# A Fourier tokenizer: last channel stored in four rings, table rows numbered by ring, chunks in a new order

## The reference, cut to what matters

```python
f = fftshift(fft2(images))                  # 64 images, 3 channels, 224 x 224
power = abs(f cropped to 192 x 192 about the centre)
idx = argsort(distance from the centre)     # 36864 points, stable
ps = power[:, :, idx].reshape(64, 3, 16, 2304)        # 16 bins by radius
tokens = einsum('bnf,ef->bne', ps of all channels per bin, W) + b
tokens = [cls, tokens] + sinusoidal positions         # 17 tokens of 192
h = layernorm(h + attention(h)); h = layernorm(h + ffn with 8 experts, top 2)
```

## Time and profile before

| | us |
|---|---|
| median of three runs | 814.05 |
| the profiled execution | 816.31 |
| its span, first to last instruction | 814.4 |
| what lies around the span | 1.9 |
| PE / DVE / POOL / ACT busy | 699.3 / 533.5 / 428.7 / 440.0 |
| transform ends (last root) | 277.2 |
| first gather, last gather issued | 287.0, 504.1 |

### The profile page before, as it was taken

One profiled execution on the slowest core, in us unless ns is written; L12 is line 12 of the kernel. 1 busy time (PEld: TensorE's weight loads), 2 busy tenths in 40 slices (PEclk: granted clock), 3 DMA queues, 4 the chain that ended last, 5 costly groups with the idle time before them and its releaser, 6 DMA issues. The chain is left out here.

```text
span 814.4 us, 22164 instructions
## 1 busy us (share of the span) xinstructions
PE 699.3 (86%) x8537; PEld 595.3 (73%) x8537; DVE 533.5 (66%) x1058; ACT 440.0 (54%) x864; POOL 428.7 (53%) x375
## 2 busy tenths in 40 slices
PE   4999999999999225788888888998899889999980
PEld 4788888888888124688787888677467677999970
DVE  3899999999999312465555555697668773555544
ACT  1788888888888512354444454232453221766640
POOL 4666677767676243777777776000200202567751
PEclk9999999999999657889999999999899965999995
DMA  9874569865996296565554554200000684233424
GB/s 244 202 194 143 149 180 259 231 186 139 266 268 269 49 228 181 152 169 155 152 145 141 147 150 136 81 2 1 1 2 2 254 252 149 37 58 58 58 29 126
DMA packets 78519, 114.90 MB, mean 141 GB/s; under 512 B 8791, under 2 KB 58108, under 8 KB 78076
## 3 DMA queue, kind: packets, MB, share of 16 engines
q1 hardware_dynamic: 61246, 76.80, 33.5%
q0 software_dynamic: 14336, 35.40, 16.8%
q10 hardware_dynamic: 2880, 1.90, 0.7%
HBM read 91.83 MB, written 22.25 MB: 140 GB/s over the span
## 5 line engine op out<-in xcount | busy, mean ns | idle before, releaser
L598 PE MATMUL psum<-power,tT 128*128 128x192 f32 x864 | 162.4, 345 | 65.4 <-DVE tT L725 65.1
L598 PEld LDWEIGHTS psum<-power,tT 128*128 128x128 f32 x864 | 148.1, 200 | 76.3 <-DVE tT L725 41.4
L539 POOL DMA_INDIRECT rows<-power_table,rank_row x144 | 146.4, 1017 | 65.9 <-issue 54.0
L725 DVE SCALAR_TENSOR_TENSOR tT<-rows,swaps,scaled 128x384 f32<-128x384 f32 x144 | 82.8, 616 | 120.7 <-ACT scaled L653 120.1
L331 PE MATMUL ps<-dft,fold 112*64 112x97 f32 (+1 forms) x3072 | 147.2, 249 | 11.6 <-POOL fold L295 11.6
L653 ACT ACTIVATE scaled<-rows,swaps 128x384 f32<-128x384 f32 x144 | 80.3, 606 | 138.8 <-DMA rows<-power_table,rank_row 135.5
L331 PEld LDWEIGHTS ps<-dft,fold 112*64 112x64 f32 (+1 forms) x3072 | 141.9, 131 | 16.6 <-issue 11.9
L302 POOL TENSOR_TENSOR ss<-uv 97x388 f32<-97x388 f32 x96 | 82.3, 880 | 76.7 <-ACT uv L373 76.7
L405 DVE TENSOR_TENSOR folded<-ps,far 112x388 f32<-112x388 f32 x192 | 98.5, 554 | 25.6 <-ACT far L361 25.5
L295 POOL TENSOR_TENSOR fold<-img 112x896 f32<-112x896 f32 x48 | 103.6, 2160 | 14.5 <-DMA img<-in_x 9.9
L422 DVE TENSOR_TENSOR uv<-ps,odd 97x388 f32<-97x388 f32 x192 | 97.8, 551 | 2.0 <-ACT odd L366 2.0
(11 more groups left out here) (174 smaller groups left out, 938.6 us busy)
## 6 DMA issues: line engine op xcount, KB each, us to landing
img<-in_x SPq DMA_DIRECT2D x48, 784.0 KB, 5.0
power_table<-power SPq DMA_DIRECT2D x16, 576.0 KB
power<-in_w_tok SPq DMA_DIRECT2D x3, 1728.0 KB, 10.3
power<-in_w SPq DMA_DIRECT2D x8, 579.0 KB, 7.3
power<-in_w SPq DMA_DIRECT2D x4, 1152.0 KB, 11.0
rows<-power_table,rank_row POOLq DMA_INDIRECT x144, 3.1
power_table<-power SPq DMA_DIRECT2D x1, 1200.0 KB
power_table<-power SPq DMA_DIRECT2D x1, 1072.0 KB, 15.4
```

What stands on the lines that cost most here:

```text
L539: pool.indirect_dma_start(out=rows[:, j % RING, half, :], out_offset=None, in_=table[0:RECORDS if j % CHUNKS < PLAIN else RECORDS + P * (L ...
L598: last = pe.matmul(ps[:, q % 2, 0:DIM], points[:, j % SWAPPED, c, s].rearrange("p h b -> p (h b)"), wt[:, c, s, chunk, :], start=(chunk == ...
L725: last = dve.scalar_tensor_tensor(out=points[:, j % SWAPPED].rearrange("p c s h b -> p (c s) h b")[:, :, half, :], in0=kept, scalar=swaps[ ...
```

## The change

Four things change together; the arithmetic is the same.

1. **Rings.** Channel 2 leaves in four rings of 816, 736, 1344 and 6513 pieces (three of 1920, 3440 and 4049 before). The rings are cut into 17 rectangles, all but the last two exactly 16 lines high.
2. **Row numbers.** Table rows are numbered rectangle after rectangle (`place_blocks`, `table_row`), with patches 0 and 1 between ring 2 and ring 3, so that a gather reads only a leading part of the table. Channels 0 and 1 are stored by the same 17 rectangles (`store_block`), two behind each image load in ring order (816, 384, 608, 640, 1120, 1536, 2656, 1648 pieces behind the eight loads, then 1).
3. **Queues.** Rectangles of rings 0 to 2 of channel 2 go in turn to SP's and ACT's queue, and the three small loads go behind ACT's. Ring 3 is SP's alone.
4. **Order.** POOL gathers bin 0 of chunks 0 to 4 (needs ring 0), bin 1 of them (ring 1), the ends of patches 0 and 1 (rings 1 and 2), the plain chunks of pair 1 (ring 2), then the joined chunks of pairs 0 and 1, and from pair 2 on as before (ring 3). The steps of the other engines that hang on this order get new places. DVE's write into `k_own`, which needs all the rings stored, now stands at step 14 (chunk 7 of pair 0 before).

```diff
+PAIRS_AHEAD = 2
...
-    assert len(patch_bin) <= PATCHES * P
-    index = rec[:, first].copy()
-    index[patch_bin, patch_pair] = RECORDS + np.arange(len(patch_bin))
+    patch_row = patch_rows(patch_bin)
+    index = table_row(rec[:, first])
+    index[patch_bin, patch_pair] = np.asarray(PATCH_AT)[patch_row // P] + patch_row % P
...
+def table_row(rec):
+    x, y = np.asarray(rec) // FREQ, np.asarray(rec) % FREQ
+    rows = np.full(x.shape, -1)
+    for ring in BLOCKS:
+        for at, (first, end, lo, hi) in ring:
+            inside = (x >= first) & (x < end) & (y >= lo) & (y < hi)
+            rows[inside] = at + ((x - first) * (hi - lo) + y - lo)[inside]
+    assert (rows >= 0).all()
+    return rows
+def patch_rows(patch_bin):
+    inner = int((patch_bin < 2 * PAIRS_AHEAD).sum())
+    rows = np.arange(len(patch_bin))
+    rows = np.where(rows < inner, rows, rows - inner + -(-inner // P) * P)
+    assert rows.max() < PATCHES * P
...
-PIECE = FREQ // PIECES
-STORES = 16 * (PIECES + 2)
-RINGS_STORED = (((0, 48, 0, 40),),
-                ((0, 48, 40, 67), (48, 80, 0, 67)),
-                ((0, 80, 67, FREQ), (80, 96, 0, FREQ), (96, FREQ, 0, FREQ - 1), (96, FREQ, FREQ - 1, FREQ)))
+RINGS_STORED = (((0, 16, 0, 28), (16, 32, 0, 23)),
+                ((0, 16, 28, 39), (16, 32, 23, 36), (32, 48, 0, 22)),
+                ((0, 16, 39, 55), (16, 32, 36, 53), (32, 48, 22, 45), (48, 64, 0, 28)),
+                ((0, 16, 55, FREQ), (16, 32, 53, FREQ), (32, 48, 45, FREQ), (48, 64, 28, FREQ), (64, 80, 0, FREQ),
+                 (80, 96, 0, FREQ), (96, FREQ, 0, FREQ - 1), (96, FREQ, FREQ - 1, FREQ)))
+STORES = 16 * sum(len(ring) for ring in RINGS_STORED)
+STORE_QUEUES = 2
+PATCHES_AHEAD = 2
+def place_blocks():
+    at, blocks, ends, patches = 0, [], [], []
+    for r, parts in enumerate(RINGS_STORED):
+        blocks.append([])
+        for first, end, lo, hi in parts:
+            blocks[r].append((at, (first, end, lo, hi)))
+            at += (end - first) * (hi - lo)
+        ends.append(at)
+        for t in range(*((0, 0), (0, 0), (0, PATCHES_AHEAD), (PATCHES_AHEAD, PATCHES))[r]):
+            patches.append(at)
+            at += P
+    assert at == ROWS
+    return blocks, ends, patches
+BLOCKS, RING_END, PATCH_AT = place_blocks()
...
+    def store_block(eng, p, block, to):
+        at, (first, end, lo, hi) = block
+        eng.dma_start(table[at:at + (end - first) * (hi - lo), p * 2 * BATCH:(p + 1) * 2 * BATCH].rearrange(
+            "(l k) e -> l k e", l=end - first),
+                      power[first:end, p % R_BUFS].rearrange("p (k e) -> p k e", k=FREQ)[:, lo:hi, :]).then_inc(to, 16)
...
-            per_load = PIECES // (at - first)
-            with sp.Fori(first // BODY_G, at // BODY_G) as body:
-                for j in range(BODY_G):
-                    load(body * BODY_G + j, j)
-                    for n in range(per_load):
-                        part_of(p, ((body * BODY_G + j - first) * per_load + n) * PIECE, PIECE, all_but_one)
-            part_of(p, PIECES * PIECE, FREQ - PIECES * PIECE, all_but_one)
-            part_of(p, 0, FREQ, last_row)
+            blocks = [block for ring in BLOCKS for block in ring]
+            per_load = len(blocks) // (at - first)
+            for g in range(first, at):
+                load(g, g)
+                for block in blocks[(g - first) * per_load:(g - first + 1) * per_load]:
+                    store_block(sp, p, block, stored[p])
+            for block in blocks[(at - first) * per_load:]:
+                store_block(sp, p, block, stored[p])
...
+    def store_ring(eng, r, mine):
+        for n, block in enumerate(BLOCKS[r]):
+            if n % STORE_QUEUES == mine or (r == len(BLOCKS) - 1 and mine == 0):
+                store_block(eng, PASSES - 1, block, ring_stored[r])
...
-STORED_OF = [int(ring_of(rank_pairs()[0][2 * q:2 * q + 2]).max()) for q in range(BINS // 2)]
+RING_OF_BIN = [int(ring_of(rank_pairs()[0][:n + 1]).max()) for n in range(BINS)]
+def chunk_order():
+    ahead = range(PAIRS_AHEAD)
+    order = [(q, chunk) for part in (range(PLAIN), range(PLAIN, CHUNKS)) for q in ahead for chunk in part]
+    return order + [(q, chunk) for q in range(PAIRS_AHEAD, BINS // 2) for chunk in range(CHUNKS)]
...
-    ENDS_AT = {1: (0,), 2: (1,), CHUNKS: (2,), CHUNKS + 1: (3,)}
-    KEEP_AT = {3: (0,), 4: (1,), CHUNKS + 2: (2,), CHUNKS + 3: (3,)}
-    def by_pairs(eng, step):
+    ORDER = chunk_order()
+    STARTS = PAIRS_AHEAD * CHUNKS
+    ENDS_AT = {PLAIN: (0, 1), STARTS + 1: (2,), STARTS + 3: (3,)}
+    KEEP_AT = {PLAIN: (0,), PLAIN + 1: (1,), STARTS + 2: (2,), STARTS + 4: (3,)}
+    FINISH_AT, TURN_AT, COPY_AT, PROJECT_AT, K_AT, Q_AT = 2, 3, 5, 6, 7, 8
+    CLS_ADD_AT, CLS_TURN_AT, CLS_COPY_AT, CLS_PROJECT_AT, CLS_Q_AT, CLS_K_AT = 4, 6, 8, 9, 11, (14, 15)
+    POSITIONS_AT = 12
+    FIRST = {"finish": STARTS - 2, "turn": STARTS - 1, "copy": STARTS + 1, "project": STARTS + 2, "k": (STARTS + 3, STARTS + 4),
+             "q": STARTS + 4}
...
-        store_ring(sp, 0)
-        for dst, src in ((b_tok[:, :], a["b_tok"].to_broadcast([P, DIM])),
-                         (cls[:, :], a["cls"].to_broadcast([BATCH, DIM])),
-                         (cls_pos[:, :], a["cls_pos"].to_broadcast([BATCH, DIM]))):
-            sp.dma_start(dst, src).then_inc(adds_in, 16)
-        store_ring(sp, 1)
-        store_ring(sp, 2)
+        for r in range(len(RINGS_STORED)):
+            store_ring(sp, r, 0)
...
-        ring_done(pool, 0)
+        landed = []
+        def ring_landed(r):
+            while len(landed) <= r:
+                ring_done(pool, len(landed))
+                landed.append(len(landed))
         def patch_ends(t):
-            ring_done(pool, PATCH_OF[t])
+            ring_landed(PATCH_OF[t])
             for e in range(2):
                 pool.indirect_dma_start(
-                    out=ends(t)[:, e, :], out_offset=None, in_=table[0:RECORDS, :],
+                    out=ends(t)[:, e, :], out_offset=None, in_=table[0:RING_END[PATCH_OF[t]], :],
                     in_offset=bass.IndirectOffsetOnAxis(
                         ap=rank_row[:, 2 * STEPS + 2 * t + e, None], axis=0)).then_inc(ends_in[t], 16)
-        def step(n, j):
-            for t in ENDS_AT.get(j, ()):
+        def gather(n, half):
+            q, chunk = ORDER[n]
+            ring_landed(RING_OF_BIN[2 * q + half])
+            pool.indirect_dma_start(
+                out=rows[:, n % RING, half, :], out_offset=None,
+                in_=table[0:RING_END[RING_OF_BIN[2 * q + half]] if chunk < PLAIN else PATCH_AT[LAST_PATCH[q]] + P, :],
+                in_offset=bass.IndirectOffsetOnAxis(ap=rank_row[:, 2 * (q * CHUNKS + chunk) + half, None], axis=0)
+            ).then_inc(gathered[n % RING], 16)
+        for half in range(2):
+            for n in range(PLAIN):
+                gather(n, half)
+        patches_known = 0
+        for n in range(PLAIN, STEPS):
+            for t in ENDS_AT.get(n, ()):
                 patch_ends(t)
-            if j % CHUNKS == 0:
-                ring_done(pool, STORED_OF[j // CHUNKS])
-            if j % CHUNKS == PLAIN:
-                for t in range(LAST_PATCH[j // CHUNKS] + 1):
-                    pool.wait_ge(patch_stored[t % 2], 16 * (t // 2 + 1))
+            q, chunk = ORDER[n]
+            while chunk >= PLAIN and patches_known <= LAST_PATCH[q]:
+                pool.wait_ge(patch_stored[patches_known % 2], 16 * (patches_known // 2 + 1))
+                patches_known += 1
             at_least(pool, points_done, n - RING + 1)
             for half in range(2):
-                pool.indirect_dma_start(
-                    out=rows[:, j % RING, half, :], out_offset=None,
-                    in_=table[0:RECORDS if j % CHUNKS < PLAIN else RECORDS + P * (LAST_PATCH[j // CHUNKS] + 1), :],
-                    in_offset=bass.IndirectOffsetOnAxis(ap=rank_row[:, 2 * j + half, None], axis=0)
-                ).then_inc(gathered[j % RING], 16)
-
-        for n in range(STEPS):
-            step(n, n)
+                gather(n, half)
...
+        for r in range(len(RINGS_STORED) - 1):
+            store_ring(act, r, 1)
+        for dst, src in ((b_tok[:, :], a["b_tok"].to_broadcast([P, DIM])),
+                         (cls[:, :], a["cls"].to_broadcast([BATCH, DIM])),
+                         (cls_pos[:, :], a["cls_pos"].to_broadcast([BATCH, DIM]))):
+            act.dma_start(dst, src).then_inc(adds_in, 16)
+        by_chunks(act, step, (first_batches, batch))
...
-            dve.wait_ge(points_used, (q + 1) * CHUNKS)
+            dve.wait_ge(points_used, STARTS - (CHUNKS - PLAIN) if isinstance(q, int) and q == 0 else (q + 1) * CHUNKS)
```

More of the change, by code:

```diff
@@ L145, in patch_use @@
     patch_bin, patch_pair = np.nonzero(~fits)
-    used = [max(np.flatnonzero(patch_bin // 2 == q), default=-1) // P for q in range(BINS // 2)]
+    tiles = patch_rows(patch_bin) // P
+    used = [max(tiles[patch_bin // 2 == q], default=-1) for q in range(BINS // 2)]
```

(50 more changed lines are left out.)

49 lines of the change are left out of this document (28 added, 21 removed).

## The result

| | before | after |
|---|---|---|
| median of 20 runs, us | 814.53 | 808.96 |
| profiled execution, us | 816.31 | 809.09 |
| its span, us | 814.4 | 807.1 |

The ratio is 0.9933, with a 95% interval of 0.9911 to 0.9955: faster by 0.7%, where 821 and slower was forecast. The time lies inside the range (799 to 837), which the share of rival A had widened downwards; the direction was wrong, and 809 lies outside the 812 to 831 of the forecast case. In the changed kernel L277 is a rectangle's store, L289 an image load, L594 and L586 POOL's gathers, L671 the token matmul, L709 a patch's store.

What follows compares the result with a forecast made beforehand. The prediction took PE to bound the transform and POOL's calls and waits to bound the gathers. Stalls of 10 and 3 us, less 6 us at the gathers, gave 821 us from 814.05, range 799 to 837.

Steps and rivals of the forecast that it cites:

- rival A: Whole kernel: the transform hides the slower stores, both stalls are 0, time 794 to 804, say 800; chance 0.34.
- the forecast case: Whole kernel: late images stall PE and the gathers gain less, 821 us with its own range 812 to 831; chance 0.48.
- the price of channels 0 and 1: Channel stores during the transform: 9409 pieces at 183 per us, less a fifth, take 41.1 us, so 22.7 us are added.
- The stall formula: PE at group 32 in the transform: load 32 at 185.5 lands at 190.5, so PE stalls 10 us, bounds 0 and 20.
- Channel 1 and the weights: Transform's end: image 47 is 3 us late, bounds 0 and 12; about 5 us of token weights precede the ring stores.
- POOL's second start: POOL goes on after waiting for patches 0 and 1, 52.5 us after the transform's end, against 45.4 before.
- The 7 us for the gathers: Ring 3 stores: 24 gather calls need 12 us of the shared engines, idle time takes 5, so 7 us are added.
- The landing behind ring 3: Patch stores before POOL goes on: they end with ring 3 and need 2.5 us to land.
- ten calls at 1.32 us: POOL's gathers after the patch wait: ten calls fewer are left, which saves 13.2 us.
- +13 -6 = +7: Whole kernel: stalls of 10 and 3 us in the transform, less 6 us at the gathers, make it slower.
- The patch wait: POOL's gathers: the long wait for the stored patches comes after its 24th call, where 14 calls were made before.
- The fewer lines, the slower: Channel stores: rectangles of 80 lines move 527 pieces per us, 48 and 32 lines 338, 16 lines 183.

## Why the prediction was wrong

**What failed first: the price of channels 0 and 1.** The step "9409 / 183 = 51.4 us, I take a fifth off" gave every piece the rate that one long rectangle has once it runs. The fifth off was my estimate, for DMA entering one rectangle while the one before still leaves. That it enters one transfer while another leaves can be seen in 165 to 167 of the changed kernel, where SP's queue moves 321 packets, 292 of them under 2 KB, of a rectangle, and 29 larger ones, of an image; no run shows a fifth saved by it. The 183 were right for long rectangles: 166 per us in 162 to 165 and 185 in 172 to 177, where the two longest rectangles of 16 lines leave, and 343 in one of 32. But the small rectangles, 3568 pieces behind the first five loads, go much faster. SP's queue in 121 to 122 of the changed kernel:

```profile
q1 hardware_dynamic: 535, 0.26, 99.2%
```

Two small rectangles leave there, 535 pieces in one microsecond. In the kernel with the rectangles reordered, where the first two lie on the same lines, it is 375, still twice the long one's rate, and 508 in 126 to 127 for two that lie 32 lines apart. The long ones start fast too and then slow down (taller rectangles, above), so a small one seems to be over before it slows; why they start fast was not settled. The overrun of channel 0 was 15.6 us, not 22.7 (bounds 9.4 and 33.0), so load 32 came at 178.4 and not at 185.5, and the transform lost 6.1 us there and not 10. I had thought that a gain could only come from neighbours on other lines. That was an assumption, and over the whole channel the kernel with them side by side was only 0.8 us later at load 32. The mechanism, a late image and a PE gap near 184, was right, as the kernel with the spread stores shows; the term was sized 1.6 times too large.

The sum had a second fault: it mixed a time (51.4 us, in which the engines are 81.5% busy) with busy times (25.6 and 14.0 us), and put the idle time after at nothing. SP's queue in 118 to 178:

```profile
q1 hardware_dynamic: 11565, 11.17, 80.6%
```

That is 48.4 us busy. Less 25.6 for the images, the stores take 22.8 us and not 41.1, and 11.6 us are idle and not 0.

**The stall formula.** It was too small, which hid part of the error. With load 32 at 178.4 it gives 178.4 + 5.0 - 178.96 - 1.7 = 2.8 us, and 6.1 came. The slack of 1.7 us was not there, since PE waited for POOL's fold of the late image, which starts beside DVE's and takes 2.88 us instead of 2.1:

```profile
183.53 2.88 POOL L336 TENSOR_TENSOR fold<-img 112x896 f32<-112x896 f32 x1 [6.33 <-DMA img<-in_x]
```

So PE stood for 4.5 us, and the granted clock of 0.50 behind the gap, of which the prediction had nothing, accounts for the rest: from 186.55 to 190.92 PE does in 4.4 us what took it 2.65 before the gap.

**Channel 1 and the weights.** 3 us were forecast and 0.4 came. The weights were issued 21.5 us after load 47 and not 31.8, and the last of them landed at 282.0, before the transform ended, so the 5 us that they were to lie in front of the rings were 0. Both follow from the first step. (Behind image 47 lie three rectangles and not two; the 7760 pieces in front of it are right.)

**POOL's second start.** 52.5 us were forecast, 48.6 came. Without the 5 us of weights the sum was 47.5, close, but two of its terms were wrong and cancelled. In 284 to 294 ACT's queue (q10) and SP's (q1) move 2810 packets, nearly the 2896 pieces of rings 0 to 2:

```profile
q10 hardware_dynamic: 1326, 0.65, 40.9%
q1 hardware_dynamic: 1484, 0.73, 38.5%
```

In 294 to 324 the rest and ring 3 leave, beside POOL's gathers (q0):

```profile
q1 hardware_dynamic: 6617, 3.33, 53.8%
q0 software_dynamic: 1361, 4.19, 38.7%
```

Rings 0 to 2 took some 9.7 us (8.6 forecast, though not because of the two queues: one gave the same start), and ring 3 some 29.7 (28.5 forecast, and 7 more for the gathers beside it). The 7 us for the gathers were too much. The landing behind ring 3, 2.5 us forecast, was 8.2: the second patch store went out at 322.24, 2 us before ring 3 had left, and needed 9.8 us, beside gathers and the positions' load. 251 pieces per us in 300 to 310 are more than the 183 of the earlier trace rows, but by count parts of at least three rectangles leave in it, with their fast starts. Deep in the last long one, in 320 to 324, it is 165 per us beside the gathers, as without them:

```profile
q1 hardware_dynamic: 661, 0.33, 45.6%
```

**The gathers' pace.** I took ten calls at 1.32 us off. The calls that remained took 1.30 us each in this profiled execution, which is 2.9 us more. But in all nine other kernels with the new order they took 1.31 to 1.33 us, so this is not shown to belong to the change.

**Sum.** +13 -6 = +7 was forecast, +6.5 -12.9 -1.0 = -7.4 came. Of the 14 us between them 6.5 are the transform, 3.9 the second start (the weights), 2.9 the pace, 1.0 the rest. The first two come from one rate applied to rectangles that it did not fit, and they are enough to turn the sign; the last two are not told from the spread of single executions. Rival A ended on the right side, but its condition, over 300 pieces per us and no stall, did not come true, nor did its 794 to 804: the change was faster with the stall in it. What rival A and the forecast both missed is that the point of balance was not "no stall": at ten calls of 1.32 us less 3.2 us, about 10 us could be lost in the transform.

**What was right.** The patch wait stays and falls after the 24th call; the DMA work in front of and beside the patch store holds it, ring 3 and then the positions (the kernels with taller rectangles, with patches at step 4 and with the positions later); and rectangles of 16 lines are what the change costs. "The fewer lines, the slower" holds for long rectangles from 32 lines to 16, 343 pieces per us against 166 to 185, and not from 64 to 32, 341 against 343. It doesn't hold for small ones: two of 16 lines reach 535 per us, 0.26 MB in one microsecond, and two on the same lines, in the kernel with the rectangles reordered, 375 (0.18 MB).

## What to carry to other kernels

A rate read from one large transfer is a rate for large transfers (183 pieces per us here, and 535 for two small ones): look for the small ones in the trace too, or keep the bound wide and let the sign hang on where the balance lies. And a rate in elapsed time, idle engines included, can't be added to busy times. Calls moved in front of a wait that has another cause are worth their whole time, less what the wait is prolonged by (13 us less 3 to 4 here, with narrow rectangles and with tall ones). And the stores of 16 partitions were paid twice here, where they ran (22.8 us of DMA for channel 0, 14.0 before) and where something else queued behind them (load 32 came 15.6 us later, and the transform ended 6.5 us later).

## What the runs showed of the hardware

Stores of 512-byte pieces in rectangles of 16 partitions settle at 166 to 185 pieces per us, in 32 partitions at 343, in 64 (told apart by count) at 341, but all of them start faster (355, 495 and about 630 per us), and two small ones of 16 reach 535. Gathers beside them did not slow this: 165 per us in 320 to 324. A second hardware queue changed neither the first gather (7.2 us after the transform, 7.0 with one queue) nor the second start (48.6 and 47.9). A patch store of 192 KB that landed in 1.9 us while DMA was little used (share 0.28 in 317.8 to 321.9 of the kernel before) needed 9.4 to 9.8 beside the end of the last ring, gathers and another load, 4.1 with taller rectangles, both patches at step 4 and the load put off; putting off the load alone brought POOL's second start 2.8 us forward. After a gap of 4.5 us PE's granted clock was 0.50 for some 3.4 us, and the same 32 matmuls took 2.24 us instead of 1.53.
